# Paged attention: half the heads scored in plain float32, two key buffers, new keys and outputs by four heads

## What is computed

```python
q = rope(rmsnorm(x @ Wq.T)); k = rope(rmsnorm(x @ Wk.T)); v = x @ Wv.T   # 32 query heads, 8 key heads, D = 128
kc = k_cache[block_table].reshape(bsz, 512, 8, 128)                     # 16 pages of 32 keys, per batch
vc = v_cache[block_table].reshape(bsz, 512, 8, 128)
k_all, v_all = concat([kc, k], axis=1), concat([vc, v], axis=1)         # 512 cached + 32 new = 544 keys
scores = where(valid, einsum('bqhd,bkhd->bhqk', q, k_all) * SCALE, -1e30)
o = einsum('bhqk,bkhd->bqhd', softmax(scores), v_all)                   # 4 query heads share a key head
x = x + o @ Wo.T
```

## Time and profile before

| | us |
|---|---|
| median of 3 runs | 2592.83 (2589.56 to 2592.96) |
| span of the profiled execution, first to last instruction | 2591.7 |
| stage_maps | about 52 to 189 |
| stage_attention, from its first DMA to the last product | about 835 to 2206 |
| stage_output | about 2210 to 2592 |

### The profile page before, as it was taken

How to read it: one execution, slowest core, us unless ns; L and a number is a source line. 1 busy time by engine, 2 the same in 40 slices (tenths; PEclk the granted TensorE clock), 3 DMA queues, 4 the chain that set the end, 5 groups by cost and what they waited for, 6 DMA issues and landing times. The chain is left out here.

```text
span 2591.7 us, 58422 instructions
## 1 busy us (share of the span) xinstructions
PE 2476.8 (96%) x16321; PEld 2107.0 (81%) x16321; DVE 2040.5 (79%) x3491; ACT 1596.5 (62%) x3675; POOL 1428.1 (55%) x1494
## 2 busy tenths in 40 slices
PE   5999999999997699999999999999999999799999
PEld 4347777777775699999999999999999999688887
DVE  3656298888887699999999999999999998332221
ACT  6664387777776576767776677676777666321111
POOL 0323144444443688888888888888888887000000
PEclk9998999999998799999999999999999999899999
DMA  9674233333323888888888888887888885744442
GB/s 312 209 229 168 85 102 102 102 102 101 102 82 92 252 268 263 258 260 263 262 264 265 268 266 266 262 258 260 263 262 265 266 268 165 216 122 123 127 128 70
DMA packets 477048, 518.20 MB, mean 200 GB/s; under 512 B 102069, under 2 KB 396981, under 8 KB 472886
## 3 DMA queue, kind: packets, MB, share of 16 engines
q1 hardware_dynamic: 426646, 340.54, 42.0%
q0 software_dynamic: 39936, 142.63, 16.6%
q10 hardware_dynamic: 10400, 34.21, 4.0%
HBM read 412.41 MB, written 104.86 MB: 200 GB/s over the span
## 5 line engine op out<-in xcount | busy, mean ns | idle before, releaser
L1163 POOL TENSOR_TENSOR att_probs<-att_probs,att_inverse 128x544 f32<-128x544 f32 x512 | 562.2, 1098 | 162.7 <-DVE att_inverse L1338 157.6
L1247 ACT ACTIVATE att_probs<-att_probs,att_low 128x544 f32<-128x544 f32 x512 | 383.3, 749 | 361.1 <-DVE att_low L1327 360.9
L1304 DVE TENSOR_TENSOR att_keys_lo<-att_keys_raw,att_keys_hi 128x512 fp32r<-128x512 f32 (+1 forms) x448 | 589.8, 1317 | 12.8 <-ACT att_keys_hi L1238 12.8
L1209 PE MATMUL att_o<-att_probs_t,att_values 128*128 128x128 f32 x4096 | 554.0, 278 | 1.0 <-ACT att_heads_out L1260 0.5
L1209 PEld LDWEIGHTS att_o<-att_probs_t,att_values 128*128 128x128 f32 x4096 | 497.8, 192 | 26.0 <-issue 6.3
L1327 DVE CUSTOM_DVE_ANT_0 att_probs<-att_score,att_mask,att_batch_cols 128x544 f32<-128x544 f32 x512 | 390.2, 762 | 20.7 <-issue 12.4
L1187 PE MATMUL att_score<-att_keys_hi,att_queries_hi 128*128 128x288 f32 (+1 forms) x1024 | 340.7, 333 | 29.1 <-DVE att_keys_lo L1304 29.1
L1140 POOL DMA_INDIRECT att_values<-L_cond_v_cache,att_v_rows_of x256 | 342.6, 1338 | 42.2 <-issue 41.1
L1238 ACT ACTIVATE att_keys_hi<-att_keys_raw 128x512 fp32r<-128x512 f32 (+1 forms) x448 | 317.4, 709 | 58.8 <-ACT att_heads_out L1260 37.8
L1334 DVE COPY att_probs_t<-att_turn 128x512 f32<-128x512 f32 x512 | 348.4, 680 | 1.4 <-PE att_turn L1195 1.3
L1195 PE MATMUL att_turn<-ident,att_probs 128*128 128x128 f32 x2048 | 325.3, 281 | 18.7 <-POOL att_probs L1163 18.7
(11 more groups left out here) (143 smaller groups left out, 4789.9 us busy)
## 6 DMA issues: line engine op xcount, KB each, us to landing
att_keys_raw<-k_cache_t SPq DMA_DIRECT2D x1024, 128.0 KB, 2.1
q_t<-proj_q_out SPq DMA_DIRECT2D x32, 1024.0 KB, 3.9
o_t<-att_heads_out ACTq DMA_DIRECT2D x64, 512.0 KB, 3.0
out_o_raw<-o_t SPq DMA_DIRECT2D x32, 1024.0 KB, 5.7
att_queries_raw<-q_t SPq DMA_DIRECT2D x63, 512.0 KB
prep_natural<-L_cond_weight SPq DMA_DIRECT2D x16, 1024.0 KB, 8.6
maps_k_nat<-L_cond_k_cache SPq DMA_DIRECT2D x16, 512.0 KB, 3.9
k_cache_t<-maps_k_turned SPq DMA_DIRECT2D x32, 256.0 KB, 3.4
```

Source lines behind the costliest of these rows:

```text
L1163: nc.gpsimd.tensor_tensor(probs[k][:], probs[k][:], inverse[k][:, 0:1].to_broadcast([P, KEYS]), ALU.mult).then_inc(probs_ready, 1)
L1209: nc.tensor.matmul(o_ps[:, 0:P], values[j][:, t, h * D:(h + 1) * D], probs_t[n % 2][:, t * P:(t + 1) * P], start=(t == 0), stop=False)
L1247: nc.scalar.activation(probs[k][:], probs[k][:], ACT.Exp, bias=low[k][:, 0:1], scale=-1.0, accum_out=total[k][:, 0:1]).then_inc(exp_done, 1)
L1304: nc.vector.tensor_tensor(keys_lo[v][:, pages], keys_raw[:, pages], f32(keys_hi[v][:, pages]), ALU.subtract).then_inc(lo_ready, 1)
```

## The change

**Key cache.** The host hands the cache over as page, d, head, key. Attention loads pages from the input directly; `stage_maps` loses the load, the eight transposes, the two copies and the stores of each group, and `k_cache_t`. SP's first wait in `stage_maps` is for a weight load (`wv_loaded`) instead of `k_loaded`.

**Scores.** Heads 0 to 3 of a batch (`NATIVE = 4`) are scored by one float32 product per column block from `keys_raw` and `queries_raw`. Heads 4 to 7 are split as before, so the split pieces hold 4 heads: five of 384 columns, one of 256, and one of 512 for the queries, which is now on DVE.

**Key buffers.** `keys_raw` and `queries_raw` are double buffered. All 18 loads of a batch (16 pages, new keys, queries) count on one semaphore, `keys_loaded[v]`. SP issues them in one go when the scores of head 4 of the batch that last used the buffer are done (two batches earlier than the one loaded). ACT waits for all 18 before the first split piece of that batch, which it makes in head 0 of the batch in between; PE waits for them before that batch's head 0.

**New keys.** Their probabilities for four heads are multiplied together (POOL, L1139, 128 x 128), turned by one transpose, kept by one copy, and multiplied by four float32 products against `new_values`, in which each head's 32 rows lie at their own place. `new_values` is loaded by four SP DMAs. The outputs of four heads collect in one PSUM bank (two banks) and are kept by one copy of 128 x 512. SP stores them, no longer ACT.

**Ring and banks.** `probs` has 8 places (was 4). The group transposes share the two `turn` banks with the others.

```diff
+            def load_keys(v, b, i, first):
...
+                if not first:
+                    sp.wait_ge(pages_loaded, 16)
+                    sp.wait_ge(scores_done[NATIVE % 2], (i - 1) * (N // 2) + v * (HK // 2) + (NATIVE // 2 + 1))
+                for n in range(NPP):
+                    sp.dma_start(keys_raw[v][:, n], kt[bass.ds(pages[n], 1)].rearrange("n d h k -> d (n h) k")).then_inc(keys_loaded[v], 16)
+                sp.dma_start(keys_raw[v][:, NPP], kn_dram[bass.ds(b, 1)].rearrange("b d h s -> d (b h) s")).then_inc(keys_loaded[v], 16)
+                sp.dma_start(queries_raw[v][:], qt_dram[:, :, bass.ds(b, 1), :].rearrange("h d b n -> d h (b n)")).then_inc(keys_loaded[v], 16)
...
+            with sp.Fori(2, PAIRS) as i:
+                load_keys(0, i * 2, i, False)
+                load_new_values(1, i * 2 - 1, i * 2 - 2, False)
+                store(1, i - 2)
+                load_keys(1, i * 2 + 1, i, False)
+                load_new_values(0, i * 2, i * 2 - 1, False)
+                store(0, i - 1)
...
                 for pages, cols in ((slice(0, FIRST), slice(LEFT, 512)), (slice(FIRST, NPP + 1), slice(512, LEFT + KEYS))):
-                    for k, (q, kt) in enumerate(((queries_hi, keys_hi), (queries_hi, keys_lo), (queries_lo, keys_hi))):
+                    if h < NATIVE:
+                        last = nc.tensor.matmul(score_ps[n % 2][:, cols], queries_raw[j][:, h, :], keys_raw[j][:, pages, h, :],
+                                                start=True, stop=True)
+                        continue
...
-                pe.wait_ge(new_ready, i * N + n)
-                nc.tensor.transpose(new_ps[0:S, 0:P], probs[n % RING][:, L:KEYS], ident[:]).then_inc(all_turned[n % RING], 1)
+                if m % GH == GH - 1:
...
+                    nc.tensor.transpose(turn_ps[job % 2][:, 0:P], new_group[g % 2].rearrange("p h s -> p (h s)"), ident[:]).then_inc(turned[job % 2], 1)
...
+                if c == 0:
+                    act.wait_ge(keys_loaded[v], i * KLD + KLD)
+                if c < NP:
+                    nc.scalar.activation(keys_hi[v][:, PARTS[c]], keys_raw[v][:, PARTS[c], NATIVE:HK], ACT.Copy).then_inc(hi_ready, 1)
```

More of the change, by code:

```diff
@@ L197, in stage_maps @@
         x3t = [a_.sb(f"x3t{u}", [P, IC, P]) for u in range(2)]
-        k_nat = a_.sb("k_nat", [P, KVD])
-        k_turned = [a_.sb(f"k_turned{q}", [P, PPT, HK // 2, PSIZE]) for q in range(2)]
         l0_ps, l1_ps, l2_ps = (a_.ps(f"l{n}") for n in range(3))
@@ L202, in stage_maps @@
         x3t_ps = a_.ps("x3t_bank")
-        k_ps = [a_.ps(f"k{q}") for q in range(2)]
+        bias_ps = a_.ps("bias_turned")
         bias_steps = a_.sem("bias_steps")
@@ L289, in _ @@
             store_x3(G // 2, -1)
-            sp.wait_ge(wv_loaded, 16)
             for u in range(2):
                 sp.wait_ge(x3_stored[u], 16 * G)
-            for q in range(2):
-                sp.wait_ge(k_stored[q], 16 * G)
         @block.gpsimd
@@ new lines, in load_keys, with load_new_values @@
+                sp.dma_start(queries_raw[v][:], qt_dram[:, :, bass.ds(b, 1), :].rearrange("h d b n -> d h (b n)")).then_inc(keys_loaded[v], 16)
+            def load_new_values(v, b, done, first):
+                if not first:
+                    sp.wait_ge(pages_loaded, 16)
+                    sp.wait_ge(o_done[1], done)
+                for q in range(GH):
+                    sp.dma_start(new_values[v][q * S:(q + 1) * S, q::GH, :],
+                                 vn_dram[bass.ds(b * S, S)].rearrange("s (h d) -> s h d", d=D)[:, q::GH, :]).then_inc(new_loaded[v], 16)
@@ L1119, in _ @@
+            store(1, PAIRS - 2)
+            store(0, PAIRS - 1)
+            store(1, PAIRS - 1)
+            for v in range(2):
+                sp.wait_ge(o_stored[v], 16 * PAIRS)
         @block.gpsimd
@@ L1342, in pair @@
                     j, h = divmod(n, HK)
-                    mask_scores(i, n)
+                    mask_scores(i, n, first)
                     if n >= 2 or not first:
@@ L1360, in _ @@
             columns(0, 0)
-            for c in range(CHUNKS):
+            for c in range(NP + 1):
                 split(0, c, 0)
```

338 lines of the change are left out of this document (159 added, 179 removed).

## The result

The changed kernel takes 2991.2 us (median of 4 runs, 2989.5 to 2996.05), the kernel before 2592.7: a ratio of 1.1546, 95% interval 1.153 to 1.1563. I had forecast 2850 with a range of 2650 to 2960. The sign and the mechanism (a closed loop over the key loads, with a clock that drops) held, the size did not: the batch takes 27.3 us where my sum had 25.1.

The account below looks back on a forecast made before the run. DVE was taken to bound the kernel (99%), PE next (94%). The sum 2592.8 - 8 (stage_maps) + 63 x (25.1 - 20.7), for late key loads and clock drops, gave 2862; forecast 2850 us, range 2650 to 2960.

Parts of the forecast that it names:

- The bounds before: Steady attention before the change: DVE 99% full, PE 94%, DMA some 78%; with DVE relieved, PE next at 19.4 us a batch.
- stage_maps: Dropping the eight key transposes per group there was to win 0.5 us each, 16 x 0.5 = 8 us.
- The loop: In attention, late key loads stall ACT's head 0, then DVE, POOL and PE, delaying the next loads: 23.9 us a batch.
- D: Time from the end of head 4's scores until all 18 key and query loads land: 16 us, between 14.5 and 16.5.
- 4.85 MB at 340 GB/s: Keys, new keys, queries and values moving together after head 4's scores: 14.3 us, plus 1.5 us before the first bytes.
- the lower end, 11.6: Landing time of the 18 loads alone: issues 9.5 us with the slower queries, plus 2.1 us to land.
- T: The end of head 4's scores on PE, when SP sends the 18 loads; ACT needs them 10.2 us later.
- The clock: PE's pause each batch halves its clock in half of the batches: 0.5 x (3 - 0.7) = +1.2 us a batch.
- PE's restart: From the loads' landing through ACT's piece, exponential, reciprocal and POOL's product until PE starts again: 2.6 us.
- D + 7.9: Batch period in attention at full clock: landing time, 2.6 us to restart PE and 5.2 us of PE work, rounded up.
- clock drops in every batch: Rival: half clock after every pause in attention, 26.2 us a batch, 2931 us; its chance lies within a shared 0.47.
- hidden: Rival: key loads in attention hidden as meant, PE bounds at 19.4 us a batch, 2509 us; chance 0.09.

Follow-up runs that it names:

- e12_four_no_values: Changed kernel with four 512 KB loads of neighbouring pages for the 16 page loads, and without cached-value loads from batch 2 on: 2508.5 us.
- e8_four_loads: Changed kernel with its 16 page loads of 128 KB replaced by four 512 KB loads of neighbouring pages: 2940.2 us.
- e4_no_values: Changed kernel with POOL's four loads of cached values left out from batch 2 on: 2756.1 us.
- e5_busy_pause: Changed kernel with 46 constant-tile transposes filling PE's pause in head 0, written to an output bank already free: 2872.1 us.
- e3_store_first: Changed kernel with SP's new-value loads and output store moved ahead of all of load_keys, including its reading of page numbers: 3197.3 us.

## Why the prediction was right and wrong

**The bounds before** were read right: with DVE relieved PE is next, at 19.4 us a batch. e12_four_no_values measures 19.45. Only the batch before was taken too short: I had 20.7 from 1327 us over 64 batches, ACT's piece comes each 20.9. A native head's scores were to take 0.93; they take 0.92 (1515.20 to 1516.12 in the changed kernel). A split head's six products take 0.84 (1533.19 to 1534.03) and start some 0.07 early against the values before them, so 0.77; the native head is 0.15 dearer, as the rows had it (0.16) and not 0.23. The group product on POOL is 0.40 us as estimated.

**stage_maps** gave 5.4 us (the first load of attention is issued at 829.21 in place of 834.64), predicted 8.

**The loop** was there in every batch, where I had put it: ACT's piece in head 0 waits for the DMA, and DVE, POOL and PE wait behind it. The signs named came out as follows: ACT idle 4 to 7 us, measured 7.8; loads landed 14 to 17 us after the wait, measured 17.5; batch 23 to 26, measured 27.3; DVE near 70% busy, measured 60%, since the batch is longer; clock under 1.00, measured 0.88. DMA is full for those 17 us in the second half only. One sign of being wrong came true: PE's turn in head 0 doesn't wait for POOL but for DVE's copy, which ends 0.24 us after POOL's product.

**What failed is the size of three terms**, 27.3 against 25.1:
- D, 17.5 in place of 16: the largest part, 1.5 us. The step that failed is "4.85 MB at 340 GB/s". What moves from the first key issue to ACT's piece is 5.3 MB at 307 GB/s (330 without the 1.5 us that I had ahead of the first bytes). The step has two faults, and both make D too short. It left out 0.65 MB that SP sends behind the keys, the store and the new values; 0.5 MB of them move in the stretch, at 340 GB/s some 1.4 us, an estimate that no run isolates. And it took the queue as full from the first byte, though the earlier trace rows had SP issue 128 KB each 0.5 us: the lower end, 11.6, was put together from these issues, but the contended case was not. e8_four_loads puts that at 1.1 us beside the values, e4_no_values against e12_four_no_values at 2.4 without them. The two overlap, and the runs do not say how the 1.5 us divide. Split the other way, the keys alone took more than I had and the values cost less: 13.8 from T in place of 11.6 (13.5 and the 0.34 to the first issue, e4_no_values), and 3.7 on top in place of 4.4. The DMA view of the changed kernel, first from 1507 to 1515 and then from 1515 to 1521 us, shows both halves:

```profile
DMA packets 1327, 1.95 MB, mean 244 GB/s; under 512 B 141, under 2 KB 1087, under 8 KB 1327
...
DMA packets 1709, 2.31 MB, mean 385 GB/s; under 512 B 188, under 2 KB 1453, under 8 KB 1709
```

- The clock. I took the drop in half of the batches, at 3 us each, less 0.7 for a shorter D: +1.2. It came in all 51 pauses looked at (the first four transposes behind each take 1.11 or 1.12 us by their row), but at 1.7 us each: PE's work from restart to T is 6.9 us in place of 5.2. That half of 3 comes near 1.7 is luck: the chance and the price were both off. D didn't get shorter, which leaves 0.5. e5_busy_pause prices the whole at 1.96 us a batch. The Trainium skill's rule (TensorE: Matmul & The Clock Gate, HAM oscillation), that such gaps return TensorE to half clock each time around, agrees with this trace: 0.88 over the stretch, and half clock behind every pause. In e4_no_values, with pauses of 2.4 us in the mean, it was 49 of 58. I had the rule and one row for it, and halved it for want of a second row.
- PE's restart, 2.86 in place of 2.6: the chain goes through DVE's copy of head 7, which I did not have in it.

1.5, 0.5 and 0.3, less the 0.1 that I had rounded up in D + 7.9, make the 2.2 us that were missing. With the batch before at 20.9 in place of 20.7 and stage_maps as measured, 2592.8 - 5.4 + 63 x (27.3 - 20.9) gives 2991.

**The rival "clock drops in every batch"** (2931) had the better mechanism, a price of 2.3 us for what measures 1.96, and the same wrong D.

**The rival "hidden"** had its threshold at D = 12.8. The runs bracket it: at 13.8 from T (e4_no_values) the loop is still there, at 11.3 (e12_four_no_values) it is gone. Its price, 2509, is what e12_four_no_values took (2508.5), to the microsecond by luck, as the batch before was 0.2 off and the first batches of that run are longer.

**The range** was cut at 2960 since I bounded D at 16.5 from above. That bound held only the rate, not the bytes I had left out nor the issues; the upper end had no row behind it.

Open: why the engines, 80% busy between 1507 and 1515 us, moved 244 GB/s there and 385 a little later. The issues can explain the idle fifth, not the slower packets.

## What to carry to other kernels

A second buffer hides a load only if what releases the load comes early enough: take the time from release to first use in the work's own order (9.7 us here), and compare it with the landing time of everything the first use waits for, with all that shares the queues in that stretch. Where it is too short, a wait for each piece or an earlier release can be worth more than a faster load: here these took 439 and 445 us off (the second with two more split heads), while four larger loads took 51 and leaving out 2.1 MB took 235. Only the last two together, in a kernel that does not load its values, took more (483). And when a wait in a loop opens a pause on PE, price the work behind the pause at half clock.

## What the runs showed of the hardware beyond that

- A pause of only 2.1 us was followed by half clock too (e4_no_values), though not at once: the first 1.4 us of work still ran at full speed. Half clock came in 49 of that run's 58 batches.
- Filling a pause with 46 useless transposes made the kernel 119 us faster, with nothing else changed.
- Sixteen page numbers take SP 5.9 us to read into registers and check. It is free in the shadow of a wait; on the path (e3_store_first) restart to issue grew by 6.9 us and the kernel by 206, although the loads then landed 3.4 us sooner.
- With no values beside them, 16 page loads of 128 KB take 13.5 us from first issue to use, 4 of 512 KB (of neighbouring pages) 11.1 for the same bytes. The Trainium skill (DMA: Bandwidth & Descriptors, Rules for kernel authors) asks for 1 MiB or more per DMA for full bandwidth; the trace agrees in direction, and 512 KB was already enough for 360 GB/s.
